# Rounded activations of a decoder layer cast to bfloat16 in place and turned tile by tile

## What is computed

```python
x = x + attn(layernorm(x), w_qkv, w_proj)      # 16 heads of 32, causal, "bitlinear" in and out
x = x + xattn(layernorm(x), k, skip, ctx, ctx) # long convolution as a Toeplitz product
x = x + ffn(layernorm(x), ...)                 # 512 -> 1536 -> 512, fp8 weights

def _act_quant(x):       # one scale for each row (position)
    s = 127.0 / clip(max(abs(x), axis=-1), 1e-05)
    return clip(round(x * s), -128.0, 127.0) / s
def _bitlinear(x, w):    # weights are -1, 0 or 1 times a scale
    return einsum('bnc,oc->bno', act_quant(x), weight_quant(w))
```

## Time and profile before

| | |
|---|---|
| Median of 3 runs | 1578.07 us (1577.15 to 1578.42) |
| Profiled execution | 1576.53 us, of which the span is 1574.7 us |
| PE busy | 1485.3 us, 94% |
| DVE busy | 1155.1 us, 73% |
| ACT busy | 713.6 us, 45% |
| POOL busy | 925.5 us, 59% |
| PE, batches in the middle of part 1 | 59.35 of 60 us |
| ACT, the same stretch | 57.23 of 60 us |

### The profile page before, as it was taken

One profiled execution on the slowest core, in us unless ns is written; L12 is line 12 of the kernel. 1 busy time (PEld: TensorE's weight loads), 2 busy tenths in 40 slices (PEclk: granted clock), 3 DMA queues, 4 the chain that ended last, 5 costly groups with the idle time before them and its releaser, 6 DMA issues.

```text
span 1574.7 us, 24008 instructions
## 1 busy us (share of the span) xinstructions
PE 1485.3 (94%) x9049; PEld 850.4 (54%) x9049; DVE 1155.1 (73%) x1821; ACT 713.6 (45%) x1252; POOL 925.5 (59%) x691
## 2 busy tenths in 40 slices
PE   2599999999986989999999999999999999999998
PEld 2477888888763444444444444444444444444443
DVE  5789999998965889986676667676677666767511
ACT  4589999999882114223223233222322322322241
POOL 2378888888884328875456445554545644555232
PEclk9899999999997999999999999999999999999999
DMA  3654646454415111112000210110200020010000
GB/s 137 156 137 124 173 132 174 127 163 130 118 62 177 40 40 47 48 54 60 21 21 21 60 27 17 51 34 14 61 21 21 21 61 27 21 34 0 2 26 27
DMA packets 58707, 105.78 MB, mean 67 GB/s; under 512 B 7624, under 2 KB 11872, under 8 KB 58592
## 3 DMA queue, kind: packets, MB, share of 16 engines
q1 hardware_dynamic: 58400, 104.10, 23.6%
q10 hardware_dynamic: 192, 0.14, 0.1%
HBM read 50.74 MB, written 19.92 MB: 45 GB/s over the span
## 4 chain that ended last, share of the span: by engine, by line
PE 77%; DVE 11%; ACT 4%; issue 4%; POOL 2%; DMA 1%; POOLq 0%; SPq 0%; DVEq 0%; ACTq 0%
PE gu L697 20%; PE gu L711 10%; PE y L662 10%; PE y L665 3%; PE y L670 3%; PE y L669 3%; PE gu L648 3%; PE y L666 3%; PE y L668 3%; PE gu L662 2%; DVE blockmax L827 2%; PE s_kq L499 2%; DVE o_sb L862 1%; PE misc L466 1%; PE s_qk L478 1%
## 5 line engine op out<-in xcount | busy, mean ns | idle before, releaser
L1578 POOL TENSOR_TENSOR fuL<-fu,fuH 128x512 f16<-128x512 f32 x96 | 126.0, 1312 | 204.2 <-ACT fuH L1381 204.2
L1480 POOL TENSOR_TENSOR pL<-pT,pH 128x768 f16<-128x768 f32 x112 | 192.8, 1722 | 51.5 <-ACT pH L1220 32.3
L662 PE MATMUL y<-kv,toep 128*128 128x512 f32 x424 | 204.1, 599 | 4.0 <-DVE kv L986 2.1
L1019 DVE TENSOR_REDUCE oT<-z 128x64 f32<-128x512 f32 x256 | 175.6, 686 | 8.8
L697 PE MATMUL gu<-fT,wg 128*128 128x512 f16 x768 | 181.4, 379 | 0.3 <-ACT fT L1404 0.3
L697 PE MATMUL gu<-fT,wu 128*128 128x512 f16 x768 | 181.4, 379 | 0.0
L1013 DVE TENSOR_TENSOR y<-y,shared 128x512 f32<-128x512 f32 x108 | 75.3, 697 | 143.4 <-PE y L670 74.1
L1015 DVE TENSOR_TENSOR z<-y,cT 128x512 f32<-128x512 f32 x236 | 162.1, 687 | 19.1 <-PE y L662 15.4
L1381 ACT ACTIVATE fuH<-fu 128x512 f16<-128x512 f32 x96 | 60.2, 627 | 206.3 <-DVE fu L1034 206.3
L711 PE MATMUL gu<-wd,fuH 128*128 128x512 f16 x384 | 145.5, 379 | 0.0
L711 PE MATMUL gu<-wd,fuL 128*128 128x512 f16 x384 | 145.5, 379 | 0.0
(11 more groups left out here) (193 smaller groups left out, 3392.8 us busy)
## 6 DMA issues: line engine op xcount, KB each, us to landing
pack<-qkhl SPq DMA_DIRECT2D x256, 128.0 KB, 2.4
x_sb<-in_x SPq DMA_DIRECT2D x16, 512.0 KB, 4.4
c_sb<-in_ctx SPq DMA_DIRECT2D x32, 256.0 KB, 3.8
hankel<-in_L_xattn_k SPq DMA_DIRECT2D x32, 256.0 KB, 3.6
x_grp<-x_scratch SPq DMA_DIRECT2D x32, 256.0 KB, 3.9
out_y<-yo SPq DMA_DIRECT2D x32, 256.0 KB, 2.8
x_scratch<-x_sb SPq DMA_DIRECT2D x15, 512.0 KB, 2.8
wraw<-in_L_attn_w_qkv SPq DMA_DIRECT2D x3, 1024.0 KB, 9.6
```

Source lines behind the costliest of these rows:

```text
L662: made = T.matmul(to, tap(h, lb - kb), keys_values(h, kb, half), start=kb == 0, stop=kb == lb)
L1019: V.tensor_reduce(out=oT[h % 2][:, lb, own].rearrange("p (b j) -> p b j", b=HB), in_=z[n % 2][:], op=ALU.add, axis=AXIS.X).then_inc(m_z, 1)
L1480: G.tensor_tensor(pL[n_split(n) % 2][:], pT[n % NPT][:], pH[n % NP][:], ALU.subtract).then_inc(low_done, 1)
L1578: G.tensor_tensor(fuL[:, ib, :], fu[n % 2][:], fuH[:, ib, :], ALU.subtract).then_inc(f_fl, 1)
```

## The change

`xn` and `o_sb` are looked at a second time as bfloat16, with a step of two elements (`xb`, `ob`), so that element i of a row of bfloat16 lies in the bytes of the float32 element i. A new instruction for each half of the rows subtracts `ROUND` and writes the whole number as bfloat16 in place: for `xn` on POOL (`cast_x`, steps 7 and 0), for `o_sb` on DVE (in `finish`, steps 2 and 3). PE turns the bfloat16 values, with the bfloat16 identity, and a call of `turn_xq` or `turn_oq` is now one half of the rows with all four blocks of channels. It waits for the cast of its own half alone. The copies out of PSUM read bfloat16 and subtract nothing. The numbers of instructions on PE and ACT stay as they are; POOL gets 32 more and DVE gets 32 more.

```diff
--- before.py
+++ after.py
@@ -135,6 +135,8 @@
         qkt = [q(f"qkt{i}", [P, 2, N], F32) for i in range(3)]
         qkhl = [q(f"qkhl{i}", [P, 2, 2, GQ, N], F16) for i in range(2)]
         xn = q("xn", [P, NT, C + 1], F32)
+
+        xb = [xn[:, t, 0:C].bitcast(BF16)[:, ::2] for t in range(NT)]
         xqT = [q(f"xqT{i}", [P, CB, N], BF16) for i in range(3)]
         diag = q("diag", [P, NT, P], F32)
         cbc = [q(f"cbc{i}", [P, N], F32) for i in range(2)]
@@ -153,6 +155,7 @@
         fw_raw = [q(f"fw_raw{i}", [P, PIECE], F32) for i in range(2)]
         fw_pow = [q(f"fw_pow{i}", [P, PIECE], F32) for i in range(2)]
         o_sb = q("o_sb", [P, NT, C + 1], F32)
+        ob = [o_sb[:, t, 0:C].bitcast(BF16)[:, ::2] for t in range(NT)]
         fw_out = q("fw_out", [P, PIECE], F16)
 
         vHL = [q(f"vHL{i}", [P, NT, HEADS - W_HEADS, VW + D], F16) for i in range(3)]
@@ -232,7 +235,7 @@
         vec_step, act_step, pool_step = signal("vec_step"), signal("act_step"), signal("pool_step")
         stats_done, var_done, shift_done, xn_done = signal("stats"), signal("var"), signal("shift"), signal("xn")
         xmax_done, c_done, inv_done = signal("xmax"), signal("c"), signal("inv")
-        xround_done, diag_done = signal("xround"), signal("diag")
+        xround_done, x_cast, diag_done = signal("xround"), signal("x_cast"), signal("diag")
         cbc_pe, cbc_done, xqT_pe, xqT_done = signal("cbc_pe"), signal("cbc"), signal("xqT_pe"), signal("xqT")
         wsum_done, wtot_pe, wscale_done = signal("wsum"), signal("wtot_pe"), signal("wscale")
         score_scale_done = signal("score_scale")
@@ -249,6 +252,7 @@
         v_whole = signal("v_whole")
         pv_pe, pv_out = signal("pv_pe"), signal("pv_out")
         o_mult, omax_done, ostep_done, oscale_done = signal("o_mult"), signal("omax"), signal("ostep"), signal("oscale")
+        o_cast = signal("o_cast")
         o_sum, o_round, c2_done = signal("o_sum"), signal("o_round"), signal("c2")
         oqT_pe, oqT_done = signal("oqT_pe"), signal("oqT")
         proj_pe, x1_done = signal("proj_pe"), signal("x1")
@@ -285,9 +289,9 @@
 
 
 
-        OUT_ROUND_AT, OUT_TURN_AT, OUT_COPY_AT, OUT_AT, X1_AT = (4, 5), (6, 7), (7, 8), (10, 11), (11, 12)
-
-        X_ROUND_AT, X_TURN_AT, X_COPY_AT = (6, 7), (8, 9), (9, 10)
+        OUT_ROUND_AT, OUT_CAST_AT, OUT_TURN_AT, OUT_COPY_AT, OUT_AT, X1_AT = (4, 5), (5, 6), (6, 7), (7, 8), (10, 11), (11, 12)
+
+        X_ROUND_AT, X_CAST_AT, X_TURN_AT, X_COPY_AT = (6, 7), (7, 8), (8, 9), (9, 10)
 
         V_AT, V_SPLIT_AT = (13, 15), (14, 16)
 
@@ -437,13 +441,12 @@
                     made = T.matmul(bank[:, t * P:(t + 1) * P], ones[:], diag[:, t, :], start=True, stop=True)
                 made.then_inc(cbc_pe, 1)
 
-            def turn_xq(b, j):
-                w.wait_ge(xround_done, NT * (b + 1))
-                bank = misc1.take(("xqT", b, j), w, (xqT_done, 2 * b + j + 1))
-                for i in range(2):
-                    cb = 2 * j + i
-                    for t in range(NT):
-                        made = T.transpose(bank[:, i * N + t * P:i * N + (t + 1) * P], xn[:, t, cb * P:(cb + 1) * P], ident[:])
+            def turn_xq(b, t):
+                w.wait_ge(const_done, C_BASE)
+                w.wait_ge(x_cast, NT * b + t + 1)
+                bank = misc1.take(("xqT", b, t), w, (xqT_done, 2 * b + t + 1))[:].bitcast(BF16)
+                for cb in range(CB):
+                    made = T.transpose(bank[:, cb * P:(cb + 1) * P], xb[t][:, cb * P:(cb + 1) * P], ident_b[:])
                 made.then_inc(xqT_pe, 1)
 
             def multiply_qk(b, g2):
@@ -540,13 +543,11 @@
                             made = T.matmul(acc[:, t, hh, :], pl[:, block, :], v, start=False, stop=mt == t)
                 made.then_inc(pv_pe, 1)
 
-            def turn_oq(b, j):
-                w.wait_ge(o_round, NT * (b + 1))
-                bank = misc1.take(("oqT", b, j), w, (oqT_done, 2 * b + j + 1))
-                for i in range(2):
-                    cb = 2 * j + i
-                    for t in range(NT):
-                        made = T.transpose(bank[:, i * N + t * P:i * N + (t + 1) * P], o_sb[:, t, cb * P:(cb + 1) * P], ident[:])
+            def turn_oq(b, t):
+                w.wait_ge(o_cast, NT * b + t + 1)
+                bank = misc1.take(("oqT", b, t), w, (oqT_done, 2 * b + t + 1))[:].bitcast(BF16)
+                for cb in range(CB):
+                    made = T.transpose(bank[:, cb * P:(cb + 1) * P], ob[t][:, cb * P:(cb + 1) * P], ident_b[:])
                 made.then_inc(oqT_pe, 1)
 
             def project_out(b, t):
@@ -869,7 +870,11 @@
                 elif k == 3:
                     w.wait_ge(ostep_done, b + 1)
                     V.reciprocal(inv, step).then_inc(oscale_done, 1)
-                elif k in X1_AT:
+                if k in OUT_CAST_AT:
+                    t = OUT_CAST_AT.index(k)
+                    w.wait_ge(o_round, NT * b + t + 1)
+                    V.tensor_scalar(ob[t], o_sb[:, t, 0:C], ROUND, None, ALU.subtract).then_inc(o_cast, 1)
+                if k in X1_AT:
                     t, xs = X1_AT.index(k), x_sb[b % NX]
                     w.wait_ge(proj_pe, 2 * b + t + 1)
                     w.wait_ge(c2_done, b + 1)
@@ -1174,8 +1179,8 @@
                 w.wait_ge(xqT_pe, 2 * b + j + 1)
                 if b >= 3:
                     w.wait_ge(v_pe, 2 * (b - 2))
-                src = misc1.of["xqT", b, j][:].rearrange("p (c n) -> p c n", c=2)
-                S.activation(xqT[b % 3][:, 2 * j:2 * j + 2, :], src, ACT.Copy, bias=-ROUND).then_inc(xqT_done, 1)
+                src = misc1.of["xqT", b, j][:].bitcast(BF16)[:, 0:CB * P].rearrange("p (c n) -> p c n", c=CB)
+                S.activation(xqT[b % 3][:, :, j * P:(j + 1) * P], src, ACT.Copy).then_inc(xqT_done, 1)
 
             def round_weights(i):
                 use = 0 if i < 3 else 1
@@ -1246,12 +1251,12 @@
                     w.wait_ge(ostep_done, b + 1)
                     S.activation(c2, step, ACT.Copy, scale=ws[:, 5:6]).then_inc(c2_done, 1)
                 if k in OUT_COPY_AT:
-                    j = OUT_COPY_AT.index(k)
-                    w.wait_ge(oqT_pe, 2 * b + j + 1)
+                    t = OUT_COPY_AT.index(k)
+                    w.wait_ge(oqT_pe, 2 * b + t + 1)
                     if b > 0:
-                        w.wait_ge(proj_pe, 2 * b)
-                    src = misc1.of["oqT", b, j][:].rearrange("p (c n) -> p c n", c=2)
-                    S.activation(oqT[:, 2 * j:2 * j + 2, :], src, ACT.Copy, bias=-ROUND).then_inc(oqT_done, 1)
+                        w.wait_ge(proj_pe, 2 * (b - 1) + t + 1)
+                    src = misc1.of["oqT", b, t][:].bitcast(BF16)[:, 0:CB * P].rearrange("p (c n) -> p c n", c=CB)
+                    S.activation(oqT[:, :, t * P:(t + 1) * P], src, ACT.Copy).then_inc(oqT_done, 1)
 
             def scale_piece(n):
                 w.wait_ge(fw_pow_done, n + 1)
@@ -1473,6 +1478,10 @@
                 G.tensor_tensor(hl[:, qk, 1, g0:g0 + 2, :], qkt[n % 3][:], hl[:, qk, 0, g0:g0 + 2, :],
                                 ALU.subtract).then_inc(qk_low, 1)
 
+            def cast_x(b, t):
+                w.wait_ge(xround_done, NT * b + t + 1)
+                G.tensor_scalar(xb[t], xn[:, t, 0:C], ROUND, None, ALU.subtract).then_inc(x_cast, 1)
+
             def low_part(n):
                 w.wait_ge(high_done, n_split(n))
                 if n_split(n) > 2:
@@ -1495,9 +1504,13 @@
                 G.tensor_tensor(fw_out[:], fw_raw[n % 2][:], fw_pow[n % 2][:], ALU.subtract).then_inc(fw_taken, 1)
 
             power_in(0)
+            for t in range(NT):
+                cast_x(0, t)
             for g2 in range(4):
                 low_qk(0, g2)
             power_in(1)
+            for t in range(NT):
+                cast_x(1, t)
 
             w.wait_ge(wtr_pe, 16)
             wT_ready(w, 3)
@@ -1517,6 +1530,9 @@
                 for b, k in batches(t, NORM_AT, LOAD_AHEAD + 11, 2):
                     if k == LOAD_AHEAD + 2:
                         power_in(b)
+                    for i in range(NT):
+                        if k == LOAD_AHEAD + X_CAST_AT[i]:
+                            cast_x(b, i)
                 if (n := piece(t, ADD_AT)) is not None:
                     add_piece(n)
                 if (n := piece(t, TAKE_AT)) is not None:
```

## The result

The changed kernel takes 1595.38 us (median of 4 executions, 1594.59 to 1597.58) against 1578.2 us for the kernel before on the same chip: a ratio of 1.0112, 95% interval 1.0095 to 1.013. It is 1.1% slower, above the range that I gave. The profiled executions have spans of 1574.7 and 1592.9 us, 18.2 us apart, and all of that lies in part 1: from the first product into `y`, which opens part 2, to the end both take 1077.1 us.

What follows compares the result with a forecast made beforehand. The loop was taken as PE 15.0, ACT 2.9 and DVE 7.6 us a period. Terms -6.6 (eleven periods), -0.4 and -0.7 (before them) and +1.4 (last two) gave -6.3 us: 1571.8 us, range 1567 to 1579.

Steps and rivals of the forecast that it cites:

- A turn 0.22 us from start to start: On PE, four bfloat16 transposes take 0.22 us instead of 0.43, saving 0.21 us a call, 0.84 us a period.
- POOL's cast, 634 ns, bound 1150 ns: A cast of xn on POOL takes 634 ns, at most 1150 ns; both hidden, as POOL idles 3.2 us a period.
- if the cover were gone, 1.2 to 2.3 us a period: Cost of POOL's casts in a middle period if they were not hidden: 1.2 to 2.3 us.
- 0.52 to 0.72 us of the turns arrive, 0.6 taken: Of PE's 0.84 us saved a period, 0.52 to 0.72 shortens it; 0.6 taken, eleven periods give -6.6 us.
- DVE's casts hidden in the middle: In steps 2 and 3 of middle periods, DVE's casts of about 0.35 us fit its idle time and cost nothing.
- +1.4 us in the last two periods: In the last two periods DVE is the chain, so two casts at 0.35 us count in full: +1.4 us.
- Before the loop, -1.1 us: Ahead of the eleven periods: -0.4 us from turns of xn in two batches, -0.7 from the second batch's turn.
- The slow rival: DVE's cast in step 3 waits for POOL's long instruction, up to 2.16 us: about +10 us, 1588 us; chance 0.12.
- The signs of being wrong: Turns not shortening, casts of step 3 over 1.3 us, or PE waiting for take_max at step 4.

Runs made afterwards that it cites:

- experiment 3: Kernel before plus seven forms of POOL instruction, each twice, ahead of the first batch, to price them; loop untouched; 1579.07 us in one execution.
- experiment 4: Changed kernel with POOL's cast of xn written as a subtraction of two tensors, the second one broadcast value; 1585.03 us, 1.0041 of the kernel before.
- version 10: Kernel without casts: ACT rounds into dense float16, PE turns float16 in two calls; 1571.76 us, 0.9955 of the kernel before.
- experiment 2: The output part alone: o_sb cast on DVE and turned as bfloat16, xn handled as in the kernel before; 1578.91 us, 1.0 of the kernel before.
- experiment 1: The input part alone: xn cast on POOL and turned as bfloat16, o_sb handled as in the kernel before; 1588.16 us, 1.0057 of the kernel before.
- experiment 6: Changed kernel with the two casts of xn a batch on DVE instead of POOL, same steps; 1600.36 us, 1.014 of the kernel before.

## Why the prediction was wrong, point by point

- **A turn 0.22 us from start to start**: right.
- **POOL's cast, 634 ns, bound 1150 ns; "Both bounds are hidden."** This is the step that failed. The true price, 1649 ns, lies outside both. I took a select of 512 elements as the nearest row because it also had one input; experiment 3 shows that the operation decides, and that a constant costs more than a second tensor. The trace before had a dearer row that I left out of the bound: L1565 in part 2, two inputs of 512 elements with float32 output, 1506 ns on average. Even so, the sentence on the bound was right: at 1040 ns the casts were hidden in the middle (experiment 4). With POOL idle for 3.2 us a period, two casts of 1.15 us fit, and two of 1.65 us fill it, and then POOL's waits for DVE count too. Measured, a period is 0.97 us longer than before and 1.25 longer than with the cheap cast. That the second lies in my "if the cover were gone, 1.2 to 2.3 us a period" is luck: those figures price two casts of 0.58 to 1.15 us in full.
- **0.52 to 0.72 us of the turns arrive, 0.6 taken**: a size a little off. Where nothing was added to POOL or DVE, 0.49 us came through (version 10, 25.49 to 25.00), and 0.30 with the output part alone, two casts on DVE included. PE's stretch to the exponential fell from 15.17 us (229.23 to 244.40) to 14.78; I had said 0.52 less.
- **DVE's casts hidden in the middle**: right, shown by the 25.18 us of experiment 2. **+1.4 us in the last two periods**: mis-sized, it was +3.8. With the output part alone one batch loses 3.1 us, where casts last up to 1.96 us and not 0.43. I had charged waits for POOL to the slow rival alone, though the earlier trace rows already had 2.1 to 2.2 us for a DVE instruction of 0.55 in those batches.
- **Before the loop, -1.1 us**: wrong, +4.5. The third batch takes 24.74 us in the changed kernel and with the input part alone, and 23.43 with the output part alone, so its 1.3 us go with POOL's casts. The rest is less sure: the output part alone, whose first cast comes long after, ended its first batch at 83.06 us against 81.47, so some 1.6 us there may be scatter.
- **The slow rival**, 1588 us, named DVE meeting POOL in step 3. Its mark, L884 over 550 ns, did appear (1501 ns), but experiment 1 has it at 553 ns and no cast on DVE, and loses 0.51 us a period: POOL is full without DVE's casts. As the main cause in the middle that rules the rival out; as the price of a cast on DVE it is real (experiment 6, and the last batches of experiment 2).
- **The signs of being wrong** were shorter turns missing, casts of step 3 over 1.3 us and a wait of PE at step 4. None of them appears in the middle of the changed kernel: the turns take 0.22 us, DVE's casts 559 ns on average, and PE has no such wait. All three looked at PE and DVE, and none at POOL.
- The Trainium skill ("GPSIMD Engine Reference", "Engine selection") calls work of one input on this engine roughly line rate. The rows disagree by their 1649 and 1489 ns beside 428 on DVE; the plain copies, 0.61 us, come nearer.

## What to carry to other kernels

A price is that of an operation and its operands, not of "one input of that size": if the trace has no row of the same operation on the same engine, take at least the dearest row of that size. Here that was 1506 ns, still below the 1649 measured, so a bound from rows alone would not have been safe. What would have warned is the price at which the plan breaks: 3.2 us of idle for two casts, 1.6 us each, hardly above that row. An engine that is least busy before can be the bound after, and once it is full, waits that cost nothing before count as well. And the best change took the work out instead of placing it: rounding into float16 needs no cast on any engine, and came out 0.5% faster than before.

## What was unexpected in the hardware

- On POOL, subtracting a constant from 512 elements took 1.49 us (1.65 in place with a step of two), subtracting a tensor 1.27, subtracting one broadcast value 1.04, copying 0.61 to 0.62.
- The same subtraction on POOL took 2.15 us instead of 1.49 beside an instruction of 128x2048 elements on DVE, which itself took 1.60 us instead of 1.22.
- ACT wrote 512 float16 values in 0.71 us densely and in 0.86 us into every second element; PE loaded such stepped two-byte tiles without loss, 0.22 us for four turns.
